# A wait on TensorE after each block's 16 gathers in a two-layer relational graph network

## The reference

```
seg = dst * NUM_REL + edge_type
sums = segment_sum(x[src], seg); cnt = segment_sum(ones, seg)
mean = (sums / max(cnt, 1)).reshape(N, 10, 128)
layer(x) = einsum('nrd,rdo->no', mean, w_rel) + x @ root + bias
out = layernorm(x + layer2(relu(layer1(x))))
```

## Time and profile before

| | |
|---|---|
| median of three runs | 5124.91 us |
| profiled execution, span from first to last instruction | 5055.0 us |
| PE, DVE, ACT busy | 2374.2, 2133.3, 981.6 us (47%, 42%, 19%) |
| POOL busy | 2978.0 us (59%), 3140 instructions |
| gathers of layer 0 in the loop | 1507, from 94.7 to 2511.6 us |
| gathers of layer 1 | 1563, from 2576.3 to 5005.2 us |

### The profile page before, as it was taken

How to read it: one execution, slowest core, us unless ns; L and a number is a source line. 1 busy time by engine, 2 the same in 40 slices (tenths; PEclk the granted TensorE clock), 3 DMA queues, 4 the chain that set the end, 5 groups by cost and what they waited for, 6 DMA issues and landing times.

```text
span 5055.0 us, 57932 instructions
## 1 busy us (share of the span) xinstructions
PE 2374.2 (47%) x13845; PEld 2115.5 (42%) x13846; DVE 2133.3 (42%) x3980; ACT 981.6 (19%) x3133; POOL 2978.0 (59%) x3140
## 2 busy tenths in 40 slices
PE   2555555555555555555634334433333333333334
PEld 2444454444444544444533333433333333333334
DVE  4444444444444444444523333333333333333335
ACT  1111121111111111211211111211121121121213
POOL 6655565655555556656545665655656666656553
PEclk6666666666766666766666666666666676666667
DMA  4222222222222222222111111111111111111111
GB/s 98 58 58 60 60 60 60 61 59 59 57 59 60 60 60 61 60 59 60 41 38 49 51 50 49 52 50 49 50 49 50 50 49 50 50 49 50 50 50 36
DMA packets 206632, 275.68 MB, mean 55 GB/s; under 512 B 62732, under 2 KB 156428, under 8 KB 206444
## 3 DMA queue, kind: packets, MB, share of 16 engines
q0 software_dynamic: 100032, 205.07, 15.6%
q1 hardware_dynamic: 101534, 67.96, 4.8%
q10 hardware_dynamic: 4878, 0.86, 0.2%
HBM read 260.85 MB, written 12.80 MB: 54 GB/s over the span
## 4 chain that ended last, share of the span: by engine, by line
another core or an unknown queue 44%; DVE 20%; issue 19%; PE 10%; DVEq 5%; ACT 1%; ACTq 0%; DMA 0%
PE ps_agg L1594 6%; DVE z_s L1894 5%; DVE S L1825 4%; DVE ring L1851 4%; DVEq L1829 3%; PE ps_y L1620 1%; PE ps_agg L1590 1%; PE ps_cnt L1579 1%; DVE cnt_ring L1842 1%; ACT prod L1499 1%; DVE hit L1816 1%; DVEq L1851 1%; DVE ahit L1790 0%; DVE amax L1788 0%
## 5 line engine op out<-in xcount | busy, mean ns | idle before, releaser
L1306 POOL DMA_INDIRECT rows<-table,idx_s x1563 | 1479.7, 947 | 1014.0 <-ACT idx_s L1458 493.9
L1306 POOL DMA_INDIRECT rows<-in_x_dram,idx_s x1507 | 1434.5, 952 | 988.3 <-ACT idx_s L1458 546.2
L1594 PE MATMUL ps_agg<-S,rows 128*128 128x140 f32 x6272 | 1371.7, 375 | 450.2 <-issue 448.7
L1594 PEld LDWEIGHTS ps_agg<-S,rows 128*128 128x128 f32 x6272 | 1317.7, 275 | 556.8 <-issue 498.0
L1851 DVE TENSOR_TENSOR ring<-ps_agg,ring 128x510 f32 x784 | 540.2, 689 | 1669.9 <-remote 1529.3
L1590 PE MATMUL ps_agg<-zero_b 128*128 128x510 bf16 x784 | 418.3, 534 | 1537.9 <-DVE ring L1851 1385.5
L1499 ACT ACTIVATE prod<-ps_y,rc_s 128x128 f32<-128x128 f32 x1960 | 555.3, 375 | 2534.0 <-remote 1850.4
L1590 PEld LDWEIGHTS ps_agg<-zero_b 128*128 128x128 bf16 x784 | 91.3, 116 | 1589.3 <-DVE ring L1851 1270.9
L1894 DVE TENSOR_REDUCE z_s<-prod 128x128 f32<-128x1536 f32 (+1 forms) x196 | 564.7, 2881 | 14.5 <-ACT prod L1502 14.5
L1825 DVE TENSOR_TENSOR S<-ps_iota,comb_t 128x1120 f32<-128x1120 f32 x392 | 516.6, 1318 | 39.3 <-issue 28.7
L1620 PE MATMUL ps_y<-wall,ring 128*128 128x128 f32 x3920 | 513.8, 289 | 14.3 <-issue 11.6
(11 more groups left out here) (111 smaller groups left out, 1095.3 us busy)
## 6 DMA issues: line engine op xcount, KB each, us to landing
attr<-in_edge_attr_dram SPq DMA_DIRECT2D x97, 336.0 KB
rows<-table,idx_s POOLq DMA_INDIRECT x1563
rows<-in_x_dram,idx_s POOLq DMA_INDIRECT x1507
x_in<-in_x_dram SPq DMA_DIRECT2D x97, 64.0 KB
table<-h_s SPq DMA_DIRECT2D x97, 64.0 KB
x_in<-table SPq DMA_DIRECT2D x97, 64.0 KB
prod<-in_x_dram SPq DMA_DIRECT2D x97, 64.0 KB
out_dram<-o_s SPq DMA_DIRECT2D x97, 64.0 KB
```

The source lines that it names most:

```text
L1306: pool.indirect_dma_start(out=rows[:, slot, j, :], out_offset=None, in_=(x, htab)[l][:, :], in_offset=bass.IndirectOffsetOnAxis(ap=at, axi ...
L1594: ins = t_.matmul(ps_agg[h][:, bass.ds(off[j] * R, TCOL)], lhsT=rows[:, o % PER, j, :], rhs=S[:, o % 2, j, :], start=False, stop=(c == 3))
```

## The change

After the gathers of the second oct of each block (odd `o`), GpSimd waits until `agg_ready` has reached the number that it has when TensorE has finished all sums of the block before the one just gathered. In loops a counting instruction (`sem_inc` on `held`) follows the wait. Nothing else is changed.

```
                             for j in range(tiles_of(o, last)):
                                 gather(l, o % PER, j, idx_s[:, o % PER, j:j + 1])
+                            if o % 2 == 1 and not (first and l == 0 and o == 1):
+
+                                pool.wait_ge(agg_ready, i * (4 * PER) + (l * QUADS + 2 * (o - 1)))
+                                if not isinstance(i, int):
+                                    pool.sem_inc(held, 1)
```

## The result

The changed kernel took **5349.37 us** (median of three runs, 5348.54 to 5359.39) against 5124.91: 4.6% slower, a ratio of 1.0456 [1.0429, 1.0482]. The forecast was 5258. The profiled execution of the changed kernel has a span of 5347.1 us and took 5349.37, so only 2.3 us lie around the span.

The account below looks back on a forecast made before the run. Bound: a run of gathers, TensorE's late signals, and whatever must happen before GpSimd restarts. Span 5055 + 283 (layer 0) - 150 (layer 1) = 5188 us; with the median 69.9 us above the span, 5258 us, range 5105 to 5520.

Parts of the forecast that it names:

- Late signals and the new chain: Both layers: TensorE's signals come about 3 us after each gather run; GpSimd's runs of 16 are then released by TensorE.
- Layer 0: Second oct's sums come behind the run: 19.7 + 3.2 + 5.0 + 0.8 = 28.7 us per block against 25.7; +283 us.
- The link that the forecast priced at 5 us: Layer 0: TensorE sums the second oct only after the run's late signals and VectorE's addition, 5.0 us per block.
- Layer 1: Second oct is summed during the run: 19.7 + 3.0 + 0.8 = 23.5 us per block against 25.0; -150 us.
- If those signals pass: Layer 1: condition that the first oct's signals get through 4.0 us into the run, against 3.3 us shown.
- It then stays so: Layer 1: once one block's second oct is executed during the run, later blocks remain ahead, at 23.5 us each.
- Blocks of the forecast kind: Layer 1: blocks whose second oct is summed inside the run of 16 gathers, 23.5 us each.
- One of the forecast's own signs: Layer 1: more gathers per 2200 us window, some 1498, against 1407 before.
- Rival B: Layer 1 never gets ahead: each block waits as in layer 0, 28.7 us, 494 us more, 5752 us; chance 10%.
- The step from span to median: Whole kernel: the median lies 69.9 us above the profiled span, so this was added to 5188 us.
- C, the wait costs nothing: Whole kernel: TensorE's pace does not depend on when GpSimd runs, so the time stays 5125 us; chance 8%.
- If the late signals have another cause than the gathers: Condition of the no-cost rival: gathers do not make TensorE's signals late, so time stays 5125 us; chance 8%.

Follow-up runs that it names:

- e5: The changed kernel itself again, beside the kernel before, on a chip with prompt signals: 3985.43 us against 3985.16, ratio 1.0000.
- e8: Changed kernel with TensorE holding each second oct until the next block's rows landed; layer 1's wait asks for the first oct; late chip: 5211.92 us against 5059.00.
- e12: Changed kernel with the wait asking only for the first oct's sums of the block before, in both layers; late chip: 5037.44 us against 5132.94, ratio 0.9815.
- e1: Changed kernel with the wait in layer 0 alone, on a prompt chip: 3976.72 us against 3977.05 for the kernel before, ratio 1.0000.
- e2: Changed kernel with the wait in layer 1 alone, on a prompt chip: 3977.17 us against 3977.05 for the kernel before, ratio 1.0002.
- e7: Changed kernel, layer 0 waiting for the first oct only, layer 1 for the block just gathered; prompt chip: 4674.40 us against 3977.33, ratio 1.1752.
- e9: Layer 0's gathers replaced by plain loads from GpSimd, without new wait; layer 1's wait one block less; prompt chip: 3670.28 us against 3976.41, ratio 0.923.
- e6: Kernel before with gathers left out; ScalarE issues plain loads of one fixed stretch of x instead; prompt chip: 2780.52 us, one run.

## Why the prediction was right and wrong

*Late signals and the new chain: right.* Signals are late during a run and come about 3 us behind its end, GpSimd is released by TensorE, and runs have 16 gathers (93 of 95 in the loop of layer 0, 81 of 90 in layer 1). In e5 the same program shows neither late signals nor a cost, so the cost hangs on them; what else differs between the chips was not separated.

*Layer 0: right.* Forecast 28.7 us per block, bounds 28.0 to 30.0; measured 29.2 here and 28.8 in e8. Pauses are 9.3 us on average, set at about 9. Last sums at 2862.1, forecast 2839: +306 us instead of +283, both against the profile of the kernel before. The link that the forecast priced at 5 us, the second oct behind the run, is the one that e12 moves away: 26.5 us per block there, on another chip. That is 2.7 us back and not 5, because the first oct is late in its place.

*Layer 1: the step that failed.* "If those signals pass" was the condition, and the forecast built on it was "It then stays so." The entry was called close: 4.0 us into the run against 3.3 us shown. It is a borderline: sums that end 2.8 us into a run are signalled at once, at 4.6 us they were not (3816.86), and at 4.9 us they were in time for the wait (3292.88). Blocks of the forecast kind do take 23.8 us (23.5 forecast), but "It then stays so" is false. A block that is early enough satisfies GpSimd's wait beforehand, and the run has 32 gathers.

Behind three of the seven such runs TensorE falls behind for one to seven blocks of 27 us (14 of the 15 such blocks); behind three others the next blocks are back at 23 to 24 us. What decides between these was not tested. Against the 23.5 us of the forecast, the 7 runs of 32 cost 38 us in all, the 15 blocks of 27.2 us 56, the 13 others 30 and the 53 at 23.8 us 14: together about the 136 us that layer 1 took beyond the forecast. First gather 2881.89 to last sums 5326.2 is 2444 us, where 2458 stood and 2308 was forecast: -14 instead of -150. One of the forecast's own signs failed with it: some 1498 gathers in 2200 us of layer 1, where 1147 in 1800 us make 1402, as many as before.

Rival B was thus partly true, with 27.2 us and not its 28.7, since the first half's signal can get through in the run (3832.69). In e8 and e12, where the wait asks for the first oct, layer 1 keeps to 23.9 and 24.1 us per block without runs of 32. It is steady there, but not ahead in the forecast's sense: the second oct comes behind the run, and no longer holds GpSimd.

*The step from span to median: wrong, and it hid part of that.* I took the 69.9 us between the span and the median as time around the span. It is 2.3 us (5349.37 against 5347.1). The kernel before was profiled at 5055.0 and ran at 5116 to 5130, and on e8's chip it ran at 5052 to 5073: the profile is of a faster execution than those of the median, on another chip or on the same, which the record does not say. In sum: 5188 + 23 (layer 0) + 136 (layer 1) = 5347; I had added 70 where 2 belonged. That the forecast was only 91 us low is partly luck: the layers were 159 us too low together, and the false step gave 68 back.

It also bears on the split. The two traces differ by 292 us (+306 and -14), the medians by 224, and the 68 us between belong to the execution profiled and not to the change. An estimate, with these 68 us spread evenly over the profile of before: about +270 us in layer 0 and -45 in layer 1.

*C, the wait costs nothing:* its condition was untrue on the first chip and true on most later ones. The sentence "If the late signals have another cause than the gathers" looked for that cause in the program, while the same program has prompt signals beside its gathers on other chips (e5). The Trainium skill, "TensorE: Matmul & The Clock Gate", "The cost: per-tile semaphore tail", has about 26 ns for each semaphore increment of a matmul. The prompt traces do not contradict it (0.21 us from the end of a half's sums to VectorE in e5); the late ones do.

*Not shown:* the split between the layers rests on the traces before and after and on e8 and e12, since e1 and e2 never ran on a late chip. Nor was a late chip seen without gathers, apart from the stretch between the layers.

## What to carry to other kernels

Before pricing a wait that ties a producer of transfers to its consumer, compare the consumer's finish with the producer's next free moment: with 13.5 us of slack it costs nothing, and with the consumer's signals late it costs what is now in line behind them. If a throttle is wanted at all, wait for the earliest event that suffices: asking for the first oct instead of both cost nothing on prompt chips, and on late ones the ratio was 0.9815 where the change had 1.0456 (one chip each, so the two were not compared on one chip). And take a profile and a median from the same chip before you subtract one from the other.

## What the runs showed of the hardware

The same program takes 3977 or 5125 us, depending on the chip. The traces of the two kinds differ in three ways:

- Semaphore updates on record: 67,500 to 67,900 on prompt chips, and 18,068 (before), 18,142 (after), 18,626 (e8) and 15,330 (e12) on late ones, for nearly the same instructions.
- TensorE's own pace while gathers run. On late chips it takes its matmul instructions one by one: in the run of 32 they start at 3310.76, 3312.86, 3315.65, 3318.45, 3321.25, 3323.36 and 3326.85, that is 2.1, 2.8 or 3.5 us apart with 0.3 to 0.4 us of work in each. On prompt chips such idle time is nil. The row of after is shown above (281.0 us <-issue), that of the kernel before has 448.7 and e8's 68.5, so its size does not go with the time. In e5 and e12 it is:

```profile
L1599 PE MATMUL ps_agg<-S,rows 128*128 128x140 f32 x6272 | 1327.4, 378 | 0.0
```

```profile
L1599 PE MATMUL ps_agg<-S,rows 128*128 128x140 f32 x6272 | 1369.6, 369 | 773.3 <-issue 768.4
```

- The granted clock, a mean between TensorE's two levels: 0.67 on the late chips of the first pair and of e12, 0.69 in e8, and 0.75 to 0.76 on prompt chips with the gathers at full pace. It does not go by the chip alone: on prompt chips it was 0.72 in e7, whose gathers pause in layer 1, 0.78 in e9 and 0.86 in e6. No run here separates it as a cause.

Fewer updates on record and a TensorE that steps slowly while gathers are issued may have one cause; no run tests it. Every timed run of the experiments has a recorded span and clock, and none was made without recording; so it is open whether the lateness comes from the recording itself or from a difference of the chips.
